# Per-item gain moved from VectorE to GpSimd, all parameter loads issued by the sync engine, and GpSimd's weight differences made a step ahead, in a two-layer routed adapter kernel

## What is computed

```
h = gelu(x @ W_down[r] + b_down[r])          1024 -> 512
u = h @ W_up[r] + b_up[r]                     512 -> 1024
y = x + u
out = (y - mean(y)) * rsqrt(var(y) + 1e-5) * gamma[r] + beta[r]
```

## Time and profile before

| what | us |
|---|---|
| median of three runs | 2822.74 |
| the profiled execution, its own time | 2828.77 |
| its span, first to last instruction | 2826.8 |
| PE busy, DVE busy | 2711.9, 2159.2 |
| ACT busy, POOL busy | 1689.6, 1422.4 |
| mean granted TensorE clock | 0.982 of full |

### The profile page before, as it was taken

One profiled execution on the slowest core, in us unless ns is written; L12 is line 12 of the kernel. 1 busy time (PEld: TensorE's weight loads), 2 busy tenths in 40 slices (PEclk: granted clock), 3 DMA queues, 4 the chain that ended last, 5 costly groups with the idle time before them and its releaser, 6 DMA issues.

```text
span 2826.8 us, 56889 instructions
## 1 busy us (share of the span) xinstructions
PE 2711.9 (96%) x11714; PEld 2216.2 (78%) x11714; DVE 2159.2 (76%) x3321; ACT 1689.6 (60%) x2907; POOL 1422.4 (50%) x956
## 2 busy tenths in 40 slices
PE   7899999998899999999989999999889999999997
PEld 5688888887788888888768888888667888888885
DVE  4677777766777777777788888888787888888886
ACT  3566666565565656666556565666555655656565
POOL 2455555555555555555454444444354444444446
PEclk9999999999999999999999999999999999999999
DMA  6565666666565656666666666656666666666663
GB/s 186 176 202 191 218 205 210 209 222 212 189 209 195 224 197 211 205 207 206 213 200 212 203 207 196 222 192 215 203 197 205 213 199 202 207 192 219 208 203 146
DMA packets 366261, 574.33 MB, mean 203 GB/s; under 512 B 41216, under 2 KB 241024, under 8 KB 365696
## 3 DMA queue, kind: packets, MB, share of 16 engines
q1 hardware_dynamic: 363968, 563.31, 61.5%
q0 software_dynamic: 1728, 6.29, 0.8%
HBM read 364.97 MB, written 204.47 MB: 201 GB/s over the span
## 4 chain that ended last, share of the span: by engine, by line
PE 82%; issue 7%; DVE 5%; POOL 1%; DVEq 1%; ACT 1%; DMA 1%; SPq 1%; POOLq 1%; ACTq 0%
PE pD L492 44%; PE bX L504 22%; PE bZ L504 16%; DVE xt L852 1%; DVE wul L769 1%; DVEq L222 1%; DVE hl L834 1%; DVE xt L875 1%; DVE wdl L752 0%; DVE xt L844 0%; DMA rwd<-in_Wd 0%; DVE xl L812 0%; POOL rwu L408 0%; POOL rwu L415 0%; ACT wdh L550 0%
## 5 line engine op out<-in xcount | busy, mean ns | idle before, releaser
L440 POOL TENSOR_TENSOR xt<-xt,cgb 128x1024 f32<-128x1024 f32 x260 | 699.8, 2692 | 342.9 <-ACT xt L662 341.6
L492 PE MATMUL pD<-wdh,xh 128*128 128x512 f32 x2080 | 818.9, 394 | 48.8 <-DVEq L796 40.4
L492 PE MATMUL pD<-wdl,xh 128*128 128x512 f32 x2080 | 815.1, 392 | 0.0
L492 PE MATMUL pD<-wdh,xl 128*128 128x512 f32 x2080 | 814.1, 391 | 0.0
L662 ACT ACTIVATE xt<-xt,rstd 128x1024 f32<-128x1024 f32 x260 | 298.9, 1150 | 383.1 <-POOL rstd L433 303.0
L492 PEld LDWEIGHTS pD<-wdh,xh 128*128 128x128 f32 x2080 | 394.6, 190 | 140.9 <-DVEq L796 49.5
L492 PEld LDWEIGHTS pD<-wdh,xl 128*128 128x128 f32 x2080 | 394.0, 189 | 83.0
L492 PEld LDWEIGHTS pD<-wdl,xh 128*128 128x128 f32 x2080 | 394.7, 190 | 81.4
L875 DVE SCALAR_TENSOR_TENSOR xt<-xt,nmean,cgb 128x1024 f32<-128x1024 f32 x260 | 441.4, 1698 | 0.0
L448 POOL TENSOR_TENSOR cs<-hT 128x256 f32<-128x256 f32 x130 | 97.1, 747 | 681.7 <-DVE hT L819 679.2
L504 PE MATMUL bX<-wuh,hh 128*128 128x512 f32 x1040 | 410.8, 395 | 27.7 <-DVE xt L844 21.5
(11 more groups left out here) (91 smaller groups left out, 3798.8 us busy)
## 6 DMA issues: line engine op xcount, KB each, us to landing
xq<-in_xB SPq DMA_DIRECT2D x130, 512.0 KB, 3.7
htok<-hg SPq DMA_DIRECT2D x260, 256.0 KB, 2.8
hq<-htok SPq DMA_DIRECT2D x1040, 64.0 KB, 2.3
xt<-in_x SPq DMA_DIRECT2D x130, 512.0 KB, 4.2
mid<-xt SPq DMA_DIRECT2D x130, 512.0 KB, 3.9
xq<-mid SPq DMA_DIRECT2D x520, 128.0 KB, 3.2
xt<-mid SPq DMA_DIRECT2D x130, 512.0 KB, 4.1
out<-xt SPq DMA_DIRECT2D x130, 512.0 KB, 2.7
```

The costliest lines, as they stand in the source:

```text
L440: eng.tensor_tensor(xt[:, k, :], xt[:, k, :], cgb[:, 1, :], ALU.add).then_inc(s_o, 1)
L492: last = eng.matmul(pD[e][:, :], a[:, e, 128 * k:128 * k + 128], w[:, k, :], start=False, stop=(k == 7 and n == 2), skip_group_check=True)
```

## The change

- **Gain.** `scale` is gone from DVE. ACT's `normal` now does the whole normalization, `x * rstd + nshift` (operation Identity with a bias), where POOL makes `rstd` times the root of 1024 and `nshift = -mean * rstd` with two more operations on 128x2 elements. POOL multiplies by gamma and then adds beta, two operations on 128x1024 for each item in place of one.
- **Loads.** SP issues the loads of the up bias (`up_biases`), of gamma and beta (`gains`), and of the whole raw down weight in one go (`down_weights`), a step ahead of use. POOL issues none.
- **Memory.** With no loads issued by POOL, 16 KB of each partition come free: `rwd` grows from 8 to 16 KB and a new tile `twu` holds two of the up weight's differences, `t2` and `t4`.
- **Differences a step ahead.** POOL makes the first two in `factors_0`, after the last `shift` of the step before, and the other two in `factors_1`, where all three were.
- **Loops.** `steps` takes a parameter `ahead`; DVE's and ACT's loop over the second layer has ten turns in place of nine.

```diff
-        rwd = sb("rwd", [128, 2, 2, K])
+        rwd = sb("rwd", [128, 8, K])
         rwu = sb("rwu", [128, 2, 2, 2, K])
+
+        twu = sb("twu", [128, 2, 2, K])
...
+        nshift = sb("nshift", [128, 4])
...
+        def steps(eng, body, low, high, ahead):
+
+            for first in (6, NP + 5):
+                for c in range(low, first):
+                    body(Pair(c))
+                turns = (first // NP * NP + NP - ahead - first) // M
+                with eng.Fori(0, turns) as j:
+                    for m in range(M):
+                        body(Pair(first + m, j))
+                low = first + M * turns
+            for c in range(low, high):
                 body(Pair(c))
...
+            def down_weights(p):
+                row, c = adapter(p), pd.next()
+                eng.wait_ge(f_rd, c + 1)
+                for h in range(2):
+                    for a in range(4):
+                        r = 256 * a + 128 * h
+                        eng.dma_start(rwd[32 * a:32 * a + 32, 4 * h:4 * h + 4, :],
+                                      Wd[row, r:r + 128, :].rearrange("a (k i) n -> (a i) k n", i=32))\
+                           .then_inc(s_rd[h], 16)
                 count(eng, s_sd, p + -1, 2, 2)
                 eng.dma_start(cbd[:, :], bd[row, :].broadcast_to([128, K])).then_inc(s_bd, 16)
 
-            def down_rest(p):
-                row, c = adapter(p), pd2.next()
-                quarter(row, c, 2)
-                quarter(row, c, 3)
+            def up_biases(p):
+                row = adapter(p)
+                count(eng, s_sx, p + -1, 1, 1)
+                eng.dma_start(cbu[:, :], bu[row, :].broadcast_to([128, H])).then_inc(s_bu, 16)
+
+            def gains(p):
+                row = adapter(p)
+                count(eng, s_o, p + -1, 2, 2)
+                eng.dma_start(cgb[:, 0, :], ga[row, :].broadcast_to([128, H])).then_inc(s_gb, 16)
+                eng.dma_start(cgb[:, 1, :], be[row, :].broadcast_to([128, H])).then_inc(s_gb, 16)
...
-            first_weights(Pair(0))
...
-                    when_new(eng, i + 1, first_weights)
+                    when_new(eng, i + 1, down_weights)
...
-                when_new(eng, i + 1, down_rest)
+                when_new(eng, u, gains)
                 if (i + 1).first():
                     up_weights(i + 1)
-
-            steps(eng, step, -1, NPH + 4)
+                    up_biases(i + 1)
+                if not v.first():
+                    when_new(eng, v, up_biases)
+
+            steps(eng, step, -1, NPH + 4, 2)
...
             def take_bu(p):
-                count(eng, s_sx, p + -1, 1, 1)
-                eng.dma_start(cbu[:, :], bu[adapter(p), :].broadcast_to([128, H])).then_inc(s_bu, 16)
-                c = pt.next()
+                eng.wait_ge(s_bu, pb.next() * 16 + 16)
+                eng.tensor_tensor(cbu[:, K:H], cbu[:, K:H], cbu[:, 0:K], ALU.subtract)
+
+            def factors_0(p):
+                c = pt[0].next()
                 eng.wait_ge(s_ru, c * 128 + 128)
                 eng.tensor_tensor(b12, b12, b11, ALU.subtract).then_inc(s_sub, 1)
-                eng.wait_ge(s_bu, c * 16 + 16)
-                eng.tensor_tensor(cbu[:, K:H], cbu[:, K:H], cbu[:, 0:K], ALU.subtract)
-
-            def factors(p):
-                c = pf.next()
-                eng.wait_ge(s_wul, c * 7 + 2)
-                eng.tensor_tensor(b12, b22, b12, ALU.subtract).then_inc(s_sub, 1)
+                eng.wait_ge(s_sub, c * 4 + 1)
+                eng.tensor_tensor(t2, b22, b12, ALU.subtract).then_inc(s_sub, 1)
+
+            def factors_1(p):
+                c = pt[1].next()
                 eng.wait_ge(s_sub, c * 4 + 2)
-                eng.tensor_tensor(b11, b12, b11, ALU.subtract).then_inc(s_sub, 1)
-                eng.wait_ge(s_wul, c * 7 + 3)
-                eng.tensor_tensor(b12, b21, b12, ALU.subtract).then_inc(s_sub, 1)
+                eng.tensor_tensor(t4, b21, t2, ALU.subtract).then_inc(s_sub, 1)
+                eng.wait_ge(s_wul, c * 7 + 1)
+                eng.tensor_tensor(b11, t2, b11, ALU.subtract).then_inc(s_sub, 1)
 
...
             def take_gb(p):
-                row = adapter(p)
-                count(eng, s_o, p + -1, 2, 2)
-                eng.dma_start(cgb[:, 0, :], ga[row, :].broadcast_to([128, H])).then_inc(s_gb, 16)
-                eng.dma_start(cgb[:, 1, :], be[row, :].broadcast_to([128, H])).then_inc(s_gb, 16)
                 eng.wait_ge(s_gb, pg.next() * 32 + 32)
-                eng.tensor_tensor(cgb[:, 0, :], cgb[:, 0, :], rooth[:, 0:1].broadcast_to([128, H]), ALU.mult)
+                eng.sem_inc(s_seen, 1)
...
                        .then_inc(s_rs, 1)
+                    count(eng, s_rs, p, 3, 1)
+                    eng.tensor_tensor(rstd[:, n:n + 2], rstd[:, n:n + 2], rooth[:, 0:1].broadcast_to([128, 2]), ALU.mult)\
+                       .then_inc(s_rs, 1)
+                    count(eng, s_rs, p, 3, 2)
+                    eng.tensor_tensor(nshift[:, n:n + 2], nmean[:, n:n + 2], rstd[:, n:n + 2], ALU.mult)\
+                       .then_inc(s_rs, 1)
 
             def shift(p, e):
                 if p.exists():
                     k = p.slot(e)
                     count(eng, s_z, p, 2, e + 1)
+                    eng.tensor_tensor(xt[:, k, :], xt[:, k, :], cgb[:, 0, :], ALU.mult).then_inc(s_g, 1)
+                    count(eng, s_g, p, 2, e + 1)
                     eng.tensor_tensor(xt[:, k, :], xt[:, k, :], cgb[:, 1, :], ALU.add).then_inc(s_o, 1)
...
             def step(i):
-                u, w = i + -3, i + -2
+                v, w, z = i + -1, i + -2, i + -4
                 sums(w)
-                norm(u + -1)
+                norm(z)
                 if w.exists():
                     when_new(eng, w, take_bu)
                     eng.drain().then_inc(s_cb, 1)
-                shift(u + -1, 0)
-                when_new(eng, w, factors)
-                shift(u + -1, 1)
-                if u.exists():
-                    when_new(eng, u, take_gb)
-                    eng.drain().then_inc(s_cg, 1)
+                if z.exists():
+                    when_new(eng, z, take_gb)
+                shift(z, 0)
+                when_new(eng, w, factors_1)
+                shift(z, 1)
+                when_new(eng, v, factors_0)
...
                 count(eng, s_Db, p + -1, 4, q + 1)
-                eng.wait_ge(s_rd[max(q - 1, 0)], c * 64 + 64)
-                eng.activation(wdh[:, 2 * q:2 * q + 2, :], rwd[:, q % 2, :, :], ACT.Copy).then_inc(s_wdh, 1)
+                eng.wait_ge(s_rd[q // 2], c * 64 + 64)
+                eng.activation(wdh[:, 2 * q:2 * q + 2, :], rwd[:, 2 * q:2 * q + 2, :], ACT.Copy).then_inc(s_wdh, 1)
...
-                high_wu(2, b12)
+                high_wu(2, t2)
                 high_wu(3, b22)
 
             def take_wu_2(p):
                 c = pg[2].next()
-                eng.wait_ge(s_sub, c * 4 + 3)
+                eng.wait_ge(s_sub, c * 4 + 4)
                 count(eng, s_P, p + -1, 7, 7)
                 high_wu(4, b11)
                 high_wu(5, b21)
-                eng.wait_ge(s_sub, c * 4 + 4)
-                high_wu(6, b12)
+                high_wu(6, t4)
...
             def normal(p, e):
                 if p.exists():
                     n, k = 2 * (p.c % 2) + e, p.slot(e)
-                    count(eng, s_rs, p, 1, 1)
-                    count(eng, s_n, p, 2, e + 1)
-                    eng.activation(xt[:, k, :], xt[:, k, :], ACT.Copy, scale=rstd[:, n:n + 1]).then_inc(s_z, 1)
+                    count(eng, s_rs, p, 3, 3)
+                    count(eng, s_sq, p, 4, 2 * e + 2)
+                    eng.activation(xt[:, k, :], xt[:, k, :], ACT.Identity, bias=nshift[:, n:n + 1],
+                                   scale=rstd[:, n:n + 1]).then_inc(s_z, 1)
...
-                eng.tensor_tensor(wdl[:, s, :], rwd[:, q % 2, :, :], wdh[:, s, :].bitcast(fp32), ALU.subtract)\
+                eng.tensor_tensor(wdl[:, s, :], rwd[:, s, :], wdh[:, s, :].bitcast(fp32), ALU.subtract)\
                    .then_inc(s_wdl, 1)
-                eng.wait_ge(s_wdl, c * 4 + (q + 1))
-                eng.sem_inc(f_rd, 1)
 
             def take_wd_0(p):
                 c = pd[0].next()
                 low_wd(c, 0)
                 low_wd(c, 1)
+                eng.wait_ge(s_wdl, c * 4 + 2)
+                eng.sem_inc(s_seen, 1)
 
             def take_wd_1(p):
                 c = pd[1].next()
                 low_wd(c, 2)
                 low_wd(c, 3)
+                eng.wait_ge(s_wdl, c * 4 + 4)
+                eng.sem_inc(f_rd, 1)
...
+                    count(eng, s_rs, u + -2, 3, 3)
...
-
-            def scale(u, e):
-                if u.exists():
-                    n, k = 2 * (u.c % 2) + e, u.slot(e)
-                    count(eng, s_sq, u, 4, 2 * e + 2)
-                    count(eng, s_cg, u, 1, 1)
-                    eng.scalar_tensor_tensor(out=xt[:, k, :], in0=xt[:, k, :], scalar=nmean[:, n:n + 1],
```

(5 more changed lines are left out.)

59 lines of the change are left out of this document (13 added, 46 removed).

## The result

The changed kernel takes 2862.0 us (median of 4 runs, 2849.8 to 2864.7) against 2822.1 us before: the ratio is 1.0132, 95% interval 1.0100 to 1.0163. I had forecast +18 us (2840.7); the measured +40 lies inside the range of 2808 to 2882, on the forecast side, and is more than twice the forecast. The sum lacks a cost, and the waits of PE tell where it lies. The profiled execution of the changed kernel has a span of 2860.2 us, 33.4 more than before.

The account below looks back on a forecast made before the run. PE was taken to bound the kernel, busy 96% of the span with 20.40 us steps; plain steps 0, turns +5, first phase -11, up weights +9, down weights 0, tail +15 gave +18 us: 2840.7 us, range 2808 to 2882.

Parts of the forecast that it names:

- The turns: Jumps back of DVE's loop: 0.7 us more at each of nine first-layer turns, second layer about even; +5 us taken.
- Plain steps, 0: Steps without a turn or weight change: still 20.40 us apart, since POOL's added passes still fit; 0 us.
- The walk through the step: First-layer step timed operation by operation: DVE waits for POOL's passes, and the next transpose_h starts 2.7 us in, not 0.8.
- the 0.5 us of room: First-layer step: transpose_h may start up to 3.2 us in before D02 is late; at 2.7 us, 0.5 us are left.
- rival B: POOL and DVE form a loop longer than a step, making D02 late in some 60 steps: +45, 2886 us; chance 0.20.
- rival A: Freed DVE pays: second-layer turns cost nothing (-16), up changes 4 us less each; -24, 2799 us; chance 0.20.
- First phase, -11: First up weights: earlier differences and whole raw down weight shrink PE's gaps, 10 us back plus 1 at the start.
- Later up weights, +9: Three later up-weight changes: POOL's six passes alternate with DVE's operations and delay the transpose; +3 us each.
- Later down weights, 0: Later down-weight changes: +2 us where low_wd meets POOL's passes, -2 where the load had been late; 0.
- Tail, +15: End of kernel, where nothing hides POOL's longer passes: two pairs' surplus of 5 us and one half-hidden; +15 us.

Follow-up runs that it names:

- two versions from the findings: Changed kernel with gamma on DVE except every sixth pair on POOL (2818.2 us), or only that pair's second half, plus earlier raw down loads (2825.3 us).
- 9 increments: Changed kernel with nine increments of an unused semaphore ahead of DVE's first loop, moving its later code 8 instructions on: 2834.9 us, ratio 1.0052.
- 113 increments: Kernel before with 113 increments of an unused semaphore ahead of DVE's loop, so layer 1's loop starts at place 452: 2849.8 us, ratio 1.0109.

## Why the prediction was wrong

The step that failed is "The turns": "I take 0.7 more for each of nine turns in the first layer: +6 ... I take +5 for turns". The excess over a plain step was 38.5 us in layer 1, of which 4.8 had been there: +34 where I had +6. I had seen the hole of 3.77 us at a turn and read it as a fixed property of a loop. By the runs above it is a wait for code, and code comes in pieces. The instruction transfers are 8192 bytes each (455 packets, 3.72 MB), and the same hole behind `var`, four instructions in, appears at start 324 of one kernel and 452 of another, 128 apart. Taking the `scale` instructions and part of the unrolled code out moved the start from 340, with 116 instructions to the next edge, to 324, with four. Then a turn waits for two pieces one after the other. The places of layer 2 do not fit a grid of 128 from there: the next edges around 1877 would be 1864 and 1992, and yet the loop that starts at 1877 stands idle behind its `var`. So two edges 128 apart are shown in layer 1; a period that holds for a whole program is not. The Trainium skill (Runtime: NRT & Kernel Launch, Instruction fetch mechanics) says that a taken branch whose target is not held forces a fetch before execution goes on, which agrees with the first hole. The Trainium skill gives blocks of 16 KiB or 256 instructions in the same section, where these runs show two edges 128 apart and transfers of 8192 bytes. The rule on branches would have told me to look, and I did not weigh it.

Step by step:

- *Plain steps, 0*: right. They stay 20.40 us apart. I had `transpose_h` at 2.7 us into a first-layer step; it is at 2.3 to 2.7. `low_x`, `low_h` 2 and `low_h` 3 are stretched to 1.8, 2.9 and 2.0 us, and gamma's pass begins 0.6 us later in its step than `shift` did, for 0.5. The small operations take 0.20 us each, as estimated; the power, which I left at 1.68, takes 1.08 there. The walk through the step and the rule that DVE and POOL exclude each other held, and the 0.5 us of room was enough; rival B did not come.
- *Turns, +5*: wrong in layer 1, as above (with eight jumps back, not the nine that I counted). In layer 2 also mis-sized, in the other direction: I had 0 or +1, it is about -9 in the changed kernel (two steps of 20.4 to 21.0 and 20.6 to 21.4 us where before one of 22.3), nearer to rival A's bound of -16. Both `scale`s had a part in it, as the two versions from the findings show.
- *First phase, -11*: half. The start is 2.0 us earlier and the first up change 3.6 shorter, -5.5. The 6.11 us gap became 3.49 (and 1.41 with 9 increments, near the 1 that I had), and the 4.58 us gap 5.00: the matmuls at half clock behind the second are all still there. These two are not PE's longest gaps of the phase, as the earlier trace rows says: its wait for the first down weights is longer, 8.39 us before and 10.80 after.
- *Later up weights, +9*: measured +2.3. Gamma on POOL costs 8 us here while POOL issues its own loads, and nothing where it does not (with the loads off POOL, gamma on DVE is 2 us slower at these steps). I had priced the passes and not the waits that POOL loses.
- *Later down weights, 0*: right as a sum (-3.4, +0.7, +2.9), and right by cancellation: +12 for gamma on POOL, -7 for the rest of the change (86.7 us with gamma on DVE against 93.3 before), and -5 between the run with 9 increments and the changed kernel, 4 of them at the first change, where the step ahead was slow already (25.0 us).
- *Tail, +15*: measured +12.4, inside its bounds. Two surpluses of 5 us and half of a third are 12.5 and not 15, so the reasoning was better than its sum. A pair's four passes follow each other without a pause; between two pairs stand the power, the small operations and 1.35 us of waiting for ACT.

By ratios the +37 us are: placement +23, gamma with the loads off POOL +12, the rest +2 (within the noise). By medians placement is 27. The change moved the loops of the other engines too, and their places were not varied; the rest of +2 leaves little room for them. Without the accident of placement the answer would have been +13 to +15, and my +18 a good forecast for a partly wrong reason: of my terms the plain steps and the tail were right in kind and size, the up changes and the turns of layer 2 were too high by 7 and about 9 us, and the first phase promised 5 us too much. The range was to take in rival B up to its price, but that price is 2886 and the range ends at 2882.

The experiments that undo one part could have misled here: taking gamma off POOL without looking at the code's place moves the loop's start too (to 328), and all 40 us might have been put on gamma.

## What to carry to other kernels

A loop on an engine whose step is tight should be looked at for its place as well as for its work: here an edit that removed instructions cost 23 to 27 us of 2835 because the loop then started a few instructions ahead of the edge of a fetched piece. Look in the trace for idle time behind a jump back, above all for a second stretch that ends with "issue", and test with harmless instructions ahead of the loop before blaming the edit. When work is moved to an engine, its own waits (here for loads that it issued itself) belong to the price: the same passes cost 26 us with them and 11 without.

## What the runs showed of the hardware

- A jump back on DVE costs a hole of 2.2 to 4.7 us. If the loop starts 4 or 16 instructions ahead of an edge (places 328 and 456), a second one of 1.7 to 3.8 us follows; with 36 in between none is seen.
- The power on 128x2 elements takes POOL 1.68 us in the step shown of before, and 1.08 us (956.63) or 0.70 us (249.49, at the turn shown) in the changed kernel, with the same shapes. The traces tell why: it waits for DVE. In the kernel before, DVE's first `scale` runs beside 129 of the 130 powers, and all of these take 1.67 us or more. In that kernel with 113 increments the `scale` is late at the eight turns of layer 1, and exactly these eight powers take 0.70 us. Beside a `low_h` of 0.68 us it is 1.08 to 1.16. So the small operation costs 0.70 us, and the rest is what DVE's operation holds it up. The rows are the `scale` in the step of the earlier trace rows, then a power at a turn with 113 increments:

```profile
955.89 1.28 DVE L875 SCALAR_TENSOR_TENSOR xt<-xt,nmean,cgb 128x1024 f32<-128x1024 f32 x1
...
255.74 0.70 POOL L433 TENSOR_TENSOR rstd<-var,mhalf 128x2 f32<-128x2 f32 x1 [5.12 <-DVE var L867]
```

- SP stands idle behind its last store of a step for 2.2 us in plain first-layer steps with gamma on POOL and 4.2 with it on DVE. The store is issued when POOL's last pass ends, so a longer POOL takes SP's slack.
